# Gate matmuls of batch 0 behind the products of their attention unit, in a three-layer Trainium2 kernel

## The reference

```
x = x + 0.5 * ffn(layernorm(x))
x = x + attn(layernorm(x))          # 16 heads, 4 key/value heads, head width 128
x = x + 0.5 * ffn(layernorm(x))

# ffn: a gate picks 4 of 32 experts for each token
logits = x2d @ gate_w.T             # 1024 x 256 by 256 x 32
_, sel = top_k(sigmoid(logits), 4)
w = softmax(logits) at sel, normalised

# attn: causal linear attention with a decay per head, in chunks
scores = (q @ k.T) * diag
o = scores @ v + (q * q_dec) @ kv   # kv: the state that the chunks before left
return o.reshape(b, s, 2048) @ wo.T
```

## Time and profile before

| | |
|---|---|
| time, median of 3 runs | 561.89 us |
| lowest and highest run | 561.28 and 562.34 us |
| span of the profiled execution | 560.4 us |
| PE busy in it | 523.7 us, 93% of the span |
| DVE, POOL, ACT busy | 334.1 us (60%), 282.0 us (50%), 162.6 us (29%) |
| attention's units 21 to 27, in the span | 318 to 377 us |

### The profile page before, as it was taken

One profiled execution on the slowest core, in us unless ns is written; L12 is line 12 of the kernel. 1 busy time (PEld: TensorE's weight loads), 2 busy tenths in 40 slices (PEclk: granted clock), 3 DMA queues, 4 the chain that ended last, 5 costly groups with the idle time before them and its releaser, 6 DMA issues.

```text
span 560.4 us, 10737 instructions
## 1 busy us (share of the span) xinstructions
PE 523.7 (93%) x3624; PEld 460.5 (82%) x3624; DVE 334.1 (60%) x940; ACT 162.6 (29%) x439; POOL 282.0 (50%) x301
## 2 busy tenths in 40 slices
PE   8789999999699999899999999999878899999977
PEld 7778888787568989799989988889867788788756
DVE  6854444444247989887667868677685444444432
ACT  4202222222234333434343333333220222222210
POOL 0045666663344766667555645455104566666420
PEclk9879999999889999999999999999997999999999
DMA  7989999777361331212121222221296522776637
GB/s 216 323 234 320 345 363 308 243 225 242 134 227 49 102 104 54 65 57 86 50 75 55 83 60 70 64 58 47 70 362 215 178 92 95 256 260 226 215 121 297
DMA packets 55233, 93.09 MB, mean 166 GB/s; under 512 B 7424, under 2 KB 37888, under 8 KB 55168
## 3 DMA queue, kind: packets, MB, share of 16 engines
q1 hardware_dynamic: 45952, 71.29, 39.2%
q0 software_dynamic: 6912, 18.88, 10.0%
q10 hardware_dynamic: 2304, 2.10, 1.1%
HBM read 79.67 MB, written 12.58 MB: 165 GB/s over the span
## 4 chain that ended last, share of the span: by engine, by line
PE 75%; DVE 9%; DMA 7%; issue 6%; POOL 2%; ACT 1%; SPq 0%; POOLq 0%; DVEq 0%
PE bank L1255 10%; PE bank L1357 9%; PE bank L1250 8%; PE bank L1411 7%; PE bank L1274 5%; PE bank L1276 5%; PE bank L1393 5%; PE bank L1368 4%; PE bank L1399 3%; PE bank L1379 3%; PE bank L1222 3%; PE bank L1139 2%; DMA decay_all<-xn_dram,ids 2%; PE bank L1125 2%; DMA shared<-z_dram 2%
## 5 line engine op out<-in xcount | busy, mean ns | idle before, releaser
L517 POOL DMA_INDIRECT decay_all<-xn_dram,ids x72 | 69.6, 966 | 109.9 <-PE bank L1222 40.2
L526 POOL DMA_INDIRECT z_dram<-probs_all,dest x72 | 70.2, 975 | 39.4 <-ACT probs_all L726 21.7
L962 DVE COPY wkv_sb<-bank 96x128 f32<-96x128 f32 x72 | 20.6, 287 | 93.1 <-PE bank L1265 93.1
L587 POOL TENSOR_TENSOR shared<-shared 128x512 f32<-128x512 f32 x39 | 50.2, 1286 | 42.9 <-DVE shared L1033 42.9
L718 ACT ACTIVATE rot<-bank 128x224 f32<-128x224 f32 x72 | 25.7, 357 | 140.8 <-PE bank L1255 140.8
L1255 PE MATMUL bank<-w_ch_sb,oT_all 128*128 128x256 f32 x256 | 65.7, 379 | 0.0
L1357 PE MATMUL bank<-split_sb 128*128 128x512 f32 x240 | 64.4, 404 | 0.3 <-POOL split_sb L559 0.3
L1411 PE MATMUL bank<-split_sb 128*128 128x256 f32 x384 | 53.5, 288 | 2.5 <-DVE split_sb L1056 2.3
L1250 PE MATMUL bank<-w_exp_sb,oT_all 128*128 128x192 f32 x256 | 52.6, 328 | 2.3 <-issue 1.2
L1411 PEld LDWEIGHTS bank<-split_sb 128*128 128x128 f32 x384 | 47.8, 190 | 3.2 <-issue 1.7
L1255 PEld LDWEIGHTS bank<-w_ch_sb,oT_all 128*128 128x128 f32 x256 | 46.9, 190 | 3.3
(11 more groups left out here) (167 smaller groups left out, 1032.7 us busy)
## 6 DMA issues: line engine op xcount, KB each, us to landing
shared<-w_up_piece SPq DMA_DIRECT2D x32, 448.0 KB, 5.3
w_exp_sb<-w_exp SPq DMA_DIRECT2D x32, 384.0 KB, 8.0
shared<-w_down_piece SPq DMA_DIRECT2D x32, 256.0 KB, 4.5
w_ch_sb<-w_ch SPq DMA_DIRECT2D x16, 384.0 KB, 5.9
shared<-z_dram SPq DMA_DIRECT2D x8, 512.0 KB, 6.1
wq_all<-wq SPq DMA_DIRECT2D x32, 128.0 KB, 2.1
decay_all<-decay SPq DMA_DIRECT2D x32, 128.0 KB, 2.2
wo_all<-wo SPq DMA_DIRECT2D x32, 128.0 KB, 2.1
```

The costliest lines, as they stand in the source:

```text
L517: pool.indirect_dma_start(out=xg[s], out_offset=None, in_=xn_dram[l][:, :], in_offset=bass.IndirectOffsetOnAxis(ap=ids[:, SEQ[t]:SEQ[t] + ...
L526: pool.indirect_dma_start(out=z_dram[l][:, :], out_offset=bass.IndirectOffsetOnAxis(ap=dest[:, SEQ[t]:SEQ[t] + 1], axis=0), in_=y_sb[s], i ...
L587: nc.gpsimd.tensor_tensor(dst, rope_a[r % 2], rope_b[r % 2], ALU.add).then_inc(roped, 1)
```

## The change

In each of the units 21, 23, 25 and 27 the two gate matmuls move from ahead of the unit's products to behind them. Their own waits and their signal stay. In all other units the loop over `early_tile(n, LOGIT_AT)` is empty, so nothing changes there.

```
@@ -1472,10 +1472,10 @@
                     pe.wait_ge(x2_copied, SB)
                     pe.wait_ge(index_ready, TT + i)
                     transpose_tile(pe, 2, i, early_xT_ps)
+                products(n)
                 for i in early_tile(n, LOGIT_AT):
                     pe.wait_ge(x2_copied, SB)
                     logits(pe, 1, i)
-                products(n)
             output(UNITS - 1)
```

## The result

The changed kernel takes 556.34 us (median; 556.02 to 557.57) where the kernel before, over the runs of both occasions, has 562.12 us (561.28 to 562.85). The ratio is 0.9886 with a 95% interval of 0.9853 to 0.9919: faster by 6.4 us of 561.89, within 4.6 to 8.3 us. The profiled execution has a span of 554.7 us, 5.7 us less than before.

The account below looks back on a forecast made before the run. PE's own work was taken to bound the kernel; hiding four gate waits would save 1.35, 1.24, 1.35 and 1.09 us, together 5.03, so 561.89 - 5.0 = 556.9 us, with a range of 555.8 to 558.5 us.

Parts of the forecast that it names:

- The bound and the releaser: PE bounds attention; its four gate waits, 4.4 us, are for ACT's copy of the turned tile.
- Readiness of the products and of the tile: Units 21 to 27: products run at once, 0.05 us spare in unit 23; copy hidden, by 0.13 us at tightest.
- The sum: Gains to the next query projection in units 21, 23, 25, 27: 1.35, 1.24, 1.35, 1.09 us, together 5.03.
- what the gate costs in its new place: Gate behind the products on PE: 0.44 us to the next start plus 0.08, 0.52 us a unit.
- its other end: Gain over the four units if the 0.08 us a unit is not a cost of the gate: 5.35 us.
- The idle column: PE's listed idle time at the gate step, 4.4 us, counted from modelled ends; by it 557.5 us.
- The scatter: Half a microsecond between runs of the kernel before, 561.28 to 562.34 us, giving the forecast its own range 556.0 to 558.0.
- The wait did not stay: Rival: PE idles as long behind the products or ahead of them, time stays 561.9 us; chance 0.05.
- The products were not what was late: Rival: late mask or state makes the gate add 0.52 us in each of four units, 564.0 us; chance 0.02.
- DVE did not take anything back: Rival: later search delays the next unit's split, rotation and mask, at most 2.0 us back, 558.9 us; chance 0.09.
- DVE's price: On DVE, 0.76 us from the split's start to the next rotation's, used to work out about 0.2 us to spare.

Follow-up runs that it names:

- e4_copy_early: Kernel before, PE's order kept, with ACT's copy of the turned tile moved ahead of the scaling of the values: 556.14 us, ratio 0.9892.
- e7_gate_twice: Changed kernel with the two gate matmuls of each of the four units issued twice: 558.42 us, ratio 0.9932 to the kernel before.
- The second, 0.9905: The changed kernel run again without edit, against the kernel before on the same chip: 556.15 us against 561.78 us.
- e5_search_twice: Changed kernel with DVE's search of the logits done twice in the four units: 556.10 us, ratio 0.9887 to the kernel before.
- e6_gate_later: Changed kernel with the gate moved behind the next unit's query projection, ahead of its scores: 558.46 us, ratio 0.9943 to the kernel before.

## Why the prediction was right or wrong

**The bound and the releaser: right, and shown.** PE set the pace, the four waits were for ACT's copy of the turned tile, and they vanish if either the gate moves or the copy does (e4_copy_early).

**Readiness of the products and of the tile: right.** The products start 1.78 behind the value projection (1.79 predicted) and 0.33 behind the transposes (0.33). The gate starts 326.26 - 324.69 = 1.57 behind the products (1.48 plus the 0.08 that I had put behind the gate). No new wait appeared in any unit.

**The sum: right in form, a term mis-sized.** Predicted were 1.35, 1.24, 1.35 and 1.09 us, 5.03 together. Measured on the trace are 1.42, 1.29, 1.42 and 1.17, 5.30. The step that failed is the 0.52 us of "what the gate costs in its new place": the gate costs 0.44 in the changed kernel, a second pair 0.44 to 0.45 (e7_gate_twice), and the gate ahead of the products without a wait the same (e4_copy_early). The prediction left open whether the 0.08 in that term belongs to the gate or to the wait. It belongs to the gate: e4_copy_early has no wait and still takes 1.56 us from the products to the projection. What was too large is the other part, the 0.44 from the waiting gate to the products; without a wait it is 0.37, so 0.07 of it was the restart after the wait, which the change takes away. So a unit gains 0.07 to 0.08 more than in my sum, about 0.3 us in four. The prediction carried 5.35 as its other end and chose the wrong one, and its reason for that end (a 0.08 that is not the gate's) does not hold either.

The idle column, which gave 4.4 us, would have been 0.9 too low. For unit 21 the parts are now known: 1.19 idle, 0.16 between the modelled end and the next start of an unbroken run, and 0.07 of the restart, together the 1.42 that was measured. The Trainium skill (Perfetto Trace Analysis, section Tensor Engine Instruction) calls the profiler's ends of matmuls estimated. The trace agrees: in the changed kernel the products of unit 21 start at 324.69, before the value projection's listed end at 322.91 + 1.95 = 324.86.

**The scatter: wrong.** I read half a microsecond of scatter off three runs of the kernel before. Twenty-five runs of it on one chip lie between 558.76 and 565.86 us, and the nine profiles differ by 2.4 us in when unit 16 starts and by 3.1 us in what follows attention. The range of 555.8 to 558.5 us left that out. The first ratio, 0.9886, came out at 555.5 us, 1.4 below the forecast: 0.3 is the mis-sized term, and for the other 1.1 the traces show nothing inside attention, so scatter is the likely reason. The second, 0.9905, comes to 561.89 x 0.9905 = 556.6 us, 0.3 below the forecast of 556.9 us and about what the mis-sized term explains. Which of the two lands inside the range is a matter of scatter, and so of luck. That the effect itself is 5.3 us rather than 6.4 rests on the traces. Why the parts outside attention scatter stays open.

**The rivals.** The wait did not stay. The products were not what was late. DVE did not take anything back: it had 0.46 us to spare where I had worked out 0.2. I had taken 0.76 from the split to the rotation as DVE's price, but that rotation started 330.39 - 328.72 = 1.67 behind the query projection, as it does in the changed kernel, so it was PE that it waited for; unhindered it takes 0.59 (e5_search_twice). That its queue decides from a later gate on was right, as e6_gate_later shows.

## What to carry to other kernels

When an instruction waits on an in-order engine and the one behind it is ready, compare whole periods (from one start to the same start a round later), not the idle column: here the four waits listed as 4.4 us were worth 5.3. Before moving the waiting work back, find who reads its result and what is queued behind that reader: moving the same two matmuls gave 5.3 us behind the products and 3.3 us one step further back, because the search on DVE holds up the split and the rotation. And a price read next to a wait is not a price in a flowing queue; take it from a place where nothing waits, and take the scatter from more than three runs before making a range narrow.

## What the runs showed of the hardware that I had not expected

An instruction on DVE that waits for nothing can start before the record of the one ahead of it ends. In the changed kernel the split starts 0.09 us before the end of the index search (327.24 against 327.14 + 0.19 = 327.33), and in e5_search_twice the rotation starts 0.59 us behind a split of 0.67. It is not so for every pair: the second part of the rotation (L1032) starts 327.89 - 327.19 = 0.70 behind the first, which is 0.68 long. What makes the difference was not tried.

And a float32 pair of matmuls with 32 columns costs 0.44 to 0.45 us on PE in each place tried where it does not wait: behind the products, ahead of them (e4_copy_early) and doubled (e7_gate_twice). That is 0.11 us for each of its four records, no less than a transpose of 128 columns (0.33 us for three records).
